# A last norm applied to rows, loads reordered, and weight preparation spread over the first two turns of a fused transformer kernel

## The reference, cut to what matters

```python
h = patches(x) @ tok_W.T + tok_b                 # 32 x 196 rows of 192
h = concatenate([h, txt], axis=1)                # 32 x 324 rows of 192
h = h + causal_rope_attention(norm(h), Wq, Wk, Wv)
z = norm(h)
xn = norm(z) * norm1_w + norm1_b
q, k, v = split(xn @ qkv_w.T + qkv_b)            # 12 heads of 16
x = z + softmax(q k^T / 4) v @ proj_w.T + proj_b
xn2 = norm(x) * norm2_w + norm2_b                # the last norm
gates = softmax(top2(xn2 @ w_gate))              # 8 experts
out = h + x + sum over e of gates_e * (gelu(xn2 @ W1_e + b1_e) @ W2_e + b2_e)
```

## Time and profile before

| | |
|---|---|
| median of 3 runs | 2673.45 us (2668.47 to 2679.84) |
| profiled execution | 2668.14 us |
| its span in the profile | 2666.3 us |
| PE matmul busy | 2423.8 us, 91% of the span |
| DVE busy | 1622.4 us, 61% |
| ACT busy | 1161.3 us, 44% |
| POOL busy | 1043.8 us, 39% |
| mean granted PE clock | 0.934 |

### The profile page before, as it was taken

How to read it: one execution, slowest core, us unless ns; L and a number is a source line. 1 busy time by engine, 2 the same in 40 slices (tenths; PEclk the granted TensorE clock), 3 DMA queues, 4 the chain that set the end, 5 groups by cost and what they waited for, 6 DMA issues and landing times. The chain is left out here.

```text
span 2666.3 us, 64384 instructions
## 1 busy us (share of the span) xinstructions
PE 2423.8 (91%) x19692; PEld 1880.4 (71%) x19692; DVE 1622.4 (61%) x4054; ACT 1161.3 (44%) x2242; POOL 1043.8 (39%) x1196
## 2 busy tenths in 40 slices
PE   3879999999999999899999999999999877989896
PEld 2755666666666666677777777777777657988886
DVE  2336888888888888866776666766666532111111
ACT  2223433444344434345555555555555532433332
POOL 1101333333333333244444444444444434555455
PEclk9568899999999999999999999999999988999998
DMA  5621123122322132425545555544553336887775
GB/s 97 176 28 21 35 40 49 31 35 36 50 34 32 35 50 38 109 73 116 113 99 106 108 114 115 108 94 103 114 109 103 97 96 198 211 224 201 215 208 127
DMA packets 251814, 263.23 MB, mean 99 GB/s; under 512 B 36156, under 2 KB 231464, under 8 KB 251752
## 3 DMA queue, kind: packets, MB, share of 16 engines
q1 hardware_dynamic: 214888, 230.18, 37.0%
q0 software_dynamic: 36864, 32.27, 6.9%
HBM read 212.43 MB, written 52.83 MB: 99 GB/s over the span
## 5 line engine op out<-in xcount | busy, mean ns | idle before, releaser
L1257 DVE TENSOR_REDUCE MX<-PS 108x2 f32<-108x648 f32 x576 | 455.7, 824 | 61.2 <-PE PS L1690 56.3
L817 POOL DMA_INDIRECT out<-big,tokn x192 | 303.9, 1583 | 479.4 <-DVE big L1408 262.5
L967 ACT ACTIVATE pool<-PS 108x648 f32<-108x648 f32 x576 | 387.6, 714 | 213.6 <-PE PS L1713 186.0
L1569 PE MATMUL PS<-WB,big 128*128 128x192 f32 x2304 | 408.3, 333 | 3.4 <-ACT big L996 3.4
L1569 PE MATMUL PS<-XE,WF 128*128 128x256 f16 x2880 | 369.6, 281 | 40.0 <-DMA WF<-w1p 26.1
L996 ACT ACTIVATE big<-PS,WF 128x256 f32<-128x256 f32 x576 | 242.1, 473 | 374.1 <-PE PS L1569 371.2
L1569 PEld LDWEIGHTS PS<-WB,big 128*128 128x128 f32 x2304 | 377.0, 192 | 28.7 <-issue 18.5
L1569 PEld LDWEIGHTS PS<-XE,WF 128*128 128x128 f16 x2880 | 278.4, 100 | 98.0 <-issue 33.0
L794 POOL DMA_INDIRECT xbuf<-XR,DST x192 | 190.7, 993 | 230.9 <-issue 187.9
L1408 DVE SCALAR_TENSOR_TENSOR big<-PS,grow,GB 128x192 f32<-128x192 f32 x192 | 71.3, 413 | 290.9 <-POOL GB L805 148.9
L1724 PE MATMUL PS<-pool,Vp 108*32 108x324 f32 x2304 | 213.9, 513 | 1.5 <-ACT pool L967 1.5
(11 more groups left out here) (209 smaller groups left out, 4163.7 us busy)
## 6 DMA issues: line engine op xcount, KB each, us to landing
WF<-w1p SPq DMA_DIRECT2D x96, 771.5 KB, 5.1
WB<-in_L_ffn_W SPq DMA_DIRECT2D x96, 576.0 KB, 6.0
ximg<-in_x SPq DMA_DIRECT2D x96, 196.0 KB, 5.3
XtR<-xbuf SPq DMA_DIRECT2D x96, 196.0 KB, 2.6
ximg<-in_x SPq DMA_DIRECT2D x96, 195.1 KB, 8.6
B2t<-in_L_ffn_b SPq DMA_DIRECT2D x96, 96.0 KB, 7.0
out<-R SPq DMA_DIRECT2D x32, 243.0 KB
w1p<-WF SPq DMA_DIRECT2D x8, 768.0 KB, 5.5
```

What stands on the lines that cost most here:

```text
L817: nc.gpsimd.indirect_dma_start(rows_out, bass.IndirectOffsetOnAxis(ap=tokn[:, i, s_:s_ + 1], axis=0), Yt[:, i, s_, :], None, bounds_check= ...
L967: nc.scalar.activation(Pr[:, at:at + 2, :], pair(("st", p))[0:TP, :, 0:T], ACT.Exp, scale=SCALE2).then_inc(S["ex"], 1)
L1257: nc.vector.tensor_reduce(MX[:, qt, g, 64 * jj:64 * jj + 64:32], pair(("s", p))[0:TP, :, 0:T], AX.X, ALU.max).then_inc(S["mx"], 1)
L1569: last = nc.tensor.matmul(out_ap, lhsT, rhs, start=(i == 0), stop=(i == len(products) - 1))
```

## The change

Four things. (1) The last norm's scale and offset are applied in `n3` to the rows, in two passes with a wait between them; W1, the gate weights and `b1` stay as they are, and PE's sums and `gateb` go. (2) SP issues the first loads in another order, with a semaphore for each use in place of two for all; the image and the text of batch 0 come early. (3) Preparation moves into the turns: turn 0 holds the attention weights (`early`), the six parts of `qkv_w` (`preps`), the round trip of the bias (`ready`), W1 parts 0 to 7 and, as its last step, the projection (`proj`); turn 1 holds W1 parts 8 to 15. The bias sums on DVE stand right before turn 0. (4) Raw weights land in `WB2` (three slots, and one area for the attention weights) and no longer in `pool1`; the `rsi` buffer becomes single, and part of the expert tables moves to `NB`.

The order of turn 0 is, after the change: emb, he, text, st0, early, is0, n0, tr1, tr1h, tr1l, qk1 0, v1, rm 0, v1e, qk1 1, rs 0, rm 1, rs 1, preps, stage 0, s1, m1, stage 1, e1, p1t, stage 2, rcp, p1e, stage 3, pv1, h1, stage 4, st1, xin, stage 5, is1, n1, stage 6, tr2, tr2h, stage 7, tr2l, hb, ready, qk2 0, xf, qkh 0, qk2 1, qkl 0, qkh 1, v2, qkl 1, qk2 2, qkh 2, qkl 2, v2e, proj. In turn 1 stage 8 stands after the first `s`, 9 before `n0`, 10 before `tr1`, 11 after `tr1l`, 12 before `rm 0`, 13 after `mx 10`, 14 after `st 0`, 15 before `m1`.

```diff
...
                and not (self.last and step in self.plan.ahead)]
-        if isinstance(self.front, int) and self.front == 0:
-            for k in range(2 * E):
-                out.insert(3 * k + 2, ("stage", k))
+        if isinstance(self.front, int) and self.front < 2:
+            if self.front == 0:
+                out.insert(out.index(("st0",)) + 1, ("early",))
+                out.insert(out.index(("s1",)), ("preps",))
+                out.insert(min(out.index(("qk2", 0)), out.index(("v2",))), ("ready",))
+                out.append(("proj",))
+            first = out.index(("s1",)) if self.front == 0 else 2
+            for k in range(E):
+                out.insert(first + (3 if self.front == 0 else 8) * k, ("stage", E * self.front + k))
...
         WB2 = sb("WB2", [128, 3, NC, D], F32)
+        attS = WB2[:, 0, :, :]
+        slot = [WB2[:, 1:3, :, :].rearrange("p r c d -> p (r c d)")[:, HID * i:HID * (i + 1)] for i in range(3)]
...
             def expert_out(e):
-                sp.wait_ge(stg_lo, low_upto(EARLY + 2 * e + 2))
+                sp.wait_ge(stg_lo, 2 * e + 2)
...
+            def bias_in():
+                sp.wait_ge(qb_ready, 1)
+                sp.dma_start(qbd.rearrange("(a p) -> p a", p=96), sred[:, 0:6], allow_slow_non_contiguous=True).then_inc(qb_out, 16)
+                sp.wait_ge(qb_out, 16)
+                for j in range(4):
+                    for a in range(2):
+                        sp.dma_start(qkb[32 * j + HD * a:32 * j + HD * a + HD, :],
+                                     qbd[0:2 * D].rearrange("(i j d) -> j d i", j=4, d=HD)[j],
+                                     allow_slow_non_contiguous=True).then_inc(qb_in, 16)
+                sp.dma_start(vrow, row(qbd[2 * D:], 96)).then_inc(vr_in, 16)
...
                     if step[0] == "stage":
-                        if step[1] + 2 < 2 * E:
-                            stage(EARLY + step[1] + 2)
-                        if step[1] % 2 == 1 and step[1] >= 3:
-                            expert_out(step[1] // 2 - 1)
+                        if step[1] % 2:
+                            expert_out(step[1] // 2)
+                        if step[1] + 3 < NSTG:
+                            stage(step[1] + 3)
+                    elif step[0] == "ready":
+                        bias_in()
                     elif step[0] == "xin":
                         if not (isinstance(item, int) and item == B - 1):
...
+            sp.dma_start(tokS, tok_w.rearrange("(a p) n -> p a n", p=96)).then_inc(tok_in, 16)
+            image(0)
+            sp.dma_start(tokb[:, :], row(tok_b, TP)).then_inc(tokb_in, 16)
+            for n, w in enumerate((wq, wk, wv)):
+                sp.dma_start(attS[:, 2 * n, :], w[0:128, :]).then_inc(att_in, 16)
+                for r in range(2):
+                    sp.dma_start(attS[64 * r:64 * r + 64, 2 * n + 1, :], w[128:D, :]).then_inc(att_in, 16)
+            sp.dma_start(qkvS, qkv_w.rearrange("(a p) n -> p a n", p=96)).then_inc(qkv_in, 16)
+            sp.dma_start(nrow, row(n1b, 96)).then_inc(n_in, 16)
+            sp.dma_start(sred[:, 0:6], qkv_b.rearrange("(a p) -> p a", p=96), allow_slow_non_contiguous=True).then_inc(n_in, 16)
+            sp.dma_start(nw[:, 0:1], column(n1w[0:128])).then_inc(nw_in, 16)
+            for r in range(2):
+                sp.dma_start(nw[64 * r:64 * r + 64, 1:2], column(n1w[128:D])).then_inc(nw_in, 16)
+            text(0)
             sp.wait_ge(pad_set, 1)
-            sp.dma_start(tokS, tok_w.rearrange("(a p) n -> p a n", p=96)).then_inc(big_in, 16)
-            sp.dma_start(qkvS, qkv_w.rearrange("(a p) n -> p a n", p=96)).then_inc(big_in, 16)
...
-            image(0)
-            sp.dma_start(nrow, n1b.rearrange("(a n) -> a n", a=1).to_broadcast([96, D])).then_inc(n_in, 16)
...
-            for i in range(4):
-                stage(i)
...
+            for k in range(3):
+                stage(k)
+            for i, v in enumerate((n2w, n2b)):
+                sp.dma_start(n2[:, i, :], row(v, TP)).then_inc(n2_in, 16)
...
             for e in range(E):
-                const_in(b1s[:, e, 0:NC], b1[e].rearrange("(c p) -> p c", p=128))
...
-            for i in range(4, EARLY + 2):
-                stage(i)
+                sp.dma_start(b1s[:, e, 0:NC], b1[e].rearrange("(c p) -> p c", p=128), allow_slow_non_contiguous=True
+                             ).then_inc(b1_in, 16)
...
-            pool.wait_ge(big_in, 128)
+            pool.wait_ge(tok_in, 16)
...
-            act.wait_ge(c_in, N_C[0])
-            for i in range(len(preps)):
-                v, hi, lo, scale = prep_view(i)
-                act.wait_ge(prep_full, i + 1)
-                nc.scalar.activation(hi, v, ACT.Identity, scale=scale).then_inc(prep_hi, 1)
...
-            for i in range(EARLY):
-                stage(i)
...
+            def prep(kind):
+                if kind == "qkv":
+                    act.wait_ge(nw_in, 48)
+                for i in PREPS[kind]:
+                    v, hi, lo, scale = prep_view(i)
+                    act.wait_ge(prep_full, i + 1)
+                    nc.scalar.activation(hi, v, ACT.Identity, scale=scale).then_inc(prep_hi, 1)
+            def attention_weights():
+                act.wait_ge(att_in, 144)
+                for v, hi, lo in early:
+                    nc.scalar.activation(hi, v, ACT.Copy).then_inc(att_hi, 1)
+            def stage(k):
+                v, hi, lo = stage_views(k)
+                act.wait_ge(stg_in[k % 3], 32 * (k // 3 + 1))
+                if k >= 6:
+                    act.wait_ge(w1_out[k // 2 % 3], 16 * (k // 2 // 3))
+                nc.scalar.activation(hi, v, ACT.Copy, scale=WSC).then_inc(stg_hi, 1)
+            prep("tok")
...
-            dve.wait_ge(big_in, 128)
-            dve.wait_ge(n_in, 48)
...
+            def bias_sums():
+                dve.wait_ge(qkv_in, 16)
+                dve.wait_ge(n_in, 32)
+                set_done(nc.vector.tensor_tensor(sprod.rearrange("p (a n) -> p a n", a=6), qkvS, wide96(nrow, 6), ALU.mult))
+                set_done(nc.vector.tensor_reduce(sred[:, 8:14], sprod.rearrange("p (a n) -> p a n", a=6), AX.X, ALU.add))
+                nc.vector.tensor_tensor(sred[:, 0:6], sred[:, 0:6], sred[:, 8:14], ALU.add).then_inc(qb_ready, 1)
...
                 dve.wait_ge(S["xl"], due("xl", b - 1, 1))
                 for t in range(NT):
-                    last = nc.vector.tensor_scalar(NB[:, t, :], X1[:, t, :], mvb[:, t, 0:1], rsb[:, t:t + 1],
-                                                   ALU.subtract, ALU.mult)
+                    last = nc.vector.scalar_tensor_tensor(NB[:, t, :], X1[:, t, :], mvb[:, t, 0:1], n2[:, 0, :],
+                                                          ALU.subtract, ALU.mult)
+                last.then_inc(S["na"], 1)
+                dve.wait_ge(S["na"], due("na", b, 1))
+                for t in range(NT):
+                    last = nc.vector.scalar_tensor_tensor(NB[:, t, :], NB[:, t, :], rsb[:, t:t + 1], n2[:, 1, :],
+                                                          ALU.mult, ALU.add)
                 last.then_inc(S["n3"], 1)
...
                 dve.wait_ge(S["gate"], due("gate", b, 1))
                 dve.wait_ge(S["pos2"], due("pos2", b - 1, 1))
-                nc.vector.tensor_tensor(L, bank(("gate",))[0:TP, 0:NT * E].rearrange("p (t e) -> p t e", e=E),
-                                        gateb[:, :].rearrange("p (a e) -> p a e", a=1).to_broadcast([TP, NT, E]),
-                                        ALU.add).then_inc(S["logit"], 1)
...
+            bias_sums()
+            dve.wait_ge(tokb_in, 16)
             run(Turn(BOTH, 0, None, None, None))
...
-            pe.wait_ge(nb_ready, 1)
-            for i in (ATT, ATT + 1):
-                pe.wait_ge(stg_in[i % 4], 32 * (i // 4 + 1))
-            nc.tensor.matmul(PS[3][0:TP, 0, 0:E], nbig[:, 0, :], slot[ATT % 4][:, 0:E], start=True, stop=False)
...
-                for c in range(NC):
-                    out_ap = PS[3][:, 1, NC * e + c:NC * e + c + 1]
-                    nc.tensor.matmul(out_ap, slot[i % 4][:, 128 * c:128 * c + 128], nw[:, 4:5], start=True, stop=False)
-                    last = nc.tensor.matmul(out_ap, slot[(i + 1) % 4][0:KB, 128 * c:128 * c + 128], nw[0:KB, 5:6],
-                                            start=False, stop=True)
-                last.then_inc(stg_mm, 1)
...
                     if kind == "stage":
-                        stage(step[1])
+                        continue
...
+                    if kind == "ready":
+                        pe.wait_ge(prep_hi, NQKV)
+                        pe.wait_ge(prep_lo, lows(NQKV))
+                        continue
+                    if kind == "proj":
+                        pe.wait_ge(proj_ready, 1)
+                        prep("proj")
                         continue
...
-            pe.wait_ge(b1_add, 1)
+            pe.wait_ge(prep_hi, len(preps))
+            pe.wait_ge(gate_in, 48)
...
```

(64 more changed lines are left out.)

273 lines of the change are left out of this document (108 added, 165 removed).

## The result

The changed kernel took 2642.59 us in the median of four runs (2635.86 to 2648.85), the kernel before 2671.59 us beside it (four runs, 2668.47 to 2679.84). The ratio is 0.988, 95% interval 0.9851 to 0.9908: faster by 29 us, where 31.8 were forecast (2641.7). Measured a second time, beside eleven runs of the kernel before, the ratio was 0.9902 (0.9882 to 0.9922).

The account below looks back on a forecast made before the run. PE was taken to set the pace in steady turns, but little in the 237 us of start and turns 0 and 1. Terms -33.9 - 2.2 + 2.7 + 1.6 = -31.8 take 2673.45 to 2641.7 us; range 2622 to 2660.

Parts of the forecast that it names:

- Term 1: Start of the kernel: with loads reordered, `he` of turn 0 starts at 28.7 instead of 62.6, -33.9 us.
- Term 2: Turn 0: b1 sums removed, preparations and bias round trip moved in, -2.2 us in sum.
- (a): Turn 0: PE's 192 one-column b1 matmuls go, -24.0 us, bounds -11.7 and -48.6.
- (c): Turn 0's end: the bias round trip waits in SP's DMA queue and stalls `qkh`, +16 us, bounds +10 and +26.
- (b): Turn 0: qkv preparations, `early` and eight W1 parts are mostly hidden, +2 us; with no cover, +8.
- (d): End of turn 0: `proj` exposed, last `qk2` at the lower clock, `b1_add` wait gone: +3.8 us, bounds +1 and +5.
- Term 3: Turn 1: eight W1 parts enter, some of them delaying steps, +2.7 us, bounds 0 and 8.2.
- Term 4: `n3` in 32 batches: +1.35 us each, mostly absorbed by DVE's idle time before `h1`, +1.6 us.
- A: Bias round trip not held up by the queue: stall 10 us or less, about 2630; chance 0.16.
- B: W1 chain lags: parts 4 to 7 each arrive 3 us later, 12 us more, 2654; chance 0.15.
- C: PE stays at 1.2 GHz in turns 0 and 1: +10 us, 2652; chance 0.10.
- D: `n3` decides: its whole 1.35 us passes to PE in 30 turns, 2680, slower; chance 0.04.

Follow-up runs that it names:

- e5: The changed kernel once more, unaltered, with a profile of another execution: 2636.45 us, ratio 0.9902.
- e4: The kernel before, with PE computing only one of the six columns of b1 sums of each expert: 2640.5 us, ratio 0.993.
- e1: The changed kernel with the bias round trip issued right behind the b1 loads, ahead of turn 0: 2618.35 us, ratio 0.9845.
- e9: e1 with the preparation of proj_w also moved, to right ahead of `n1` in turn 0: 2614.0 us, ratio 0.9798.
- e11: e9 with `n3` in one pass, the last norm's scale and offset left out: 2615.51 us, ratio 0.9794.
- e12: e9 with the first pass of `n3` moved ahead of `m1` in the attention turns: 2615.41 us, ratio 0.9791.
- e3: The changed kernel with 16 filler instructions at the head of ACT's program: 2632.81 us in a single execution.
- e8: The changed kernel with the first pass of `n3` done twice: 2646.83 us in a single execution.

## Why the prediction was right

**Term 1, -33.9, measured -34.0** (62.63 to 28.60; the other profiles of kernels with this start have 26.9 to 28.6). Two of its parts were off and cancelled: `emb` starts at 19.9, not 18, for the image landed later; and DVE's sums end at 27.4, not 28.6. So PE set `he`; in e5 the two end within 0.1 us of each other, and `he` starts at 26.9. That the term came out to 0.1 us is luck; its mechanism, loads in the order of use, is what the trace shows. The bound of 26.2 that I gave for hidden sums rested on the 18.

**Term 2, -2.2, measured -6.1**, 88.4 in both profiles of the changed kernel. (a) -24.0 against -26.4 by e4 (20.0 measured, 6.4 estimated); of the 24.0 only the last block's 11.7 had rows behind it. (c) +16 against +15.6, by which `qm` came earlier in e1; its inner times were 76.3 for 80.5 (issue), 14.4 for 13 (the store), 4.8 for 5.5 (the way back). (b) and (d) were never separated in full: with the others measured, -6.1 + 26.4 - 15.6 = +4.7 is left for them where I had 5.8, and 2.1 of it went with the stall in e1 (17.7 us in all). e9 (less the 2.8 us of clock), e11 and e12 put the part of `proj` at 1.2 to 2.6 us.

The queue in front of the store was the reason for (c)'s size, as argued from the earlier trace rows: 7.0, 9.3, 14.4 us with nothing, W1 transfers, and image and W1 transfers ahead. The Trainium skill (DMA: Bandwidth & Descriptors, Queues, rings and completion order) has each DMA engine work through a queue in ring order; by that rule a small store waits for what stands ahead of it, and all three runs agree. But 7.0 of the 14.4 us were there with no large transfer ahead of it, and some 5 passed in all three with the DMA engines idle, so moving the trip, not emptying the queue, is the cure.

**Term 3, +2.7, measured +1.6 in the mean**: turn 1 took 77.9 to 84.5 us in the twelve profiles with eight parts in it, 81.6 in the mean (83.3 and 84.0 for the changed kernel), against 80.0 in the one profile of before. That is too wide to confirm the parts of the term. The scatter is the clock: 78.0 us went with a granted clock of 0.74 and 58.4 us of busy PE (e3), 84.0 with 0.65 and 65.1 (e5).

**Term 4, +1.6, measured some 4 in the attention turns**, and between 0 and 15 us by the ratios of whole kernels: its size is not settled. That DVE's gap takes the pass in was right in each kind of turn, and so were the 0.1 us left over in 16 turns (25.71 for 25.62 us at `h1`), though by two slips that cancel: 1.35 less the gap of 1.17 is 0.18 and not 0.1, and the pass added 1.18. The rest of the 4 us is the mix of clock stretches, which I had not foreseen.

**The sum.** Profile of before to e5's profile the span fell by 31.4 us, nearly the forecast's 31.8, and by 19.3 to the first profile. The medians give 29.0 beside the first measurement and 24.2 beside e5, where the kernel before ran faster (2660.6) than in its profile (2668.1). The terms as measured add up to some -34.5. So the mechanisms of terms 1 and 2, nearly all of the forecast, are shown, and the total to some 5 to 10 us; that 31.8 and 29.0 lie so close is in part luck. The test that I had set, steady turns lengthened by 0.5 us or more, called the prediction wrong on the first profile (55.07 for 54.30) and not on e5's; only the repeat clears term 4.

**The rivals.** A (trip not held up) is excluded by 14.4 against 7.0. B (W1 chain lags, 12 us): with the bias trip out of the way turn 0 took 70.7 us, against 71.5 expected without any lag. C (PE stays at 1.2 GHz): turn 0 and 1 had 0.61 and 0.67, against 0.60 and 0.66; e4, with the sums nearly gone, had 0.63 and 0.73. The Trainium skill (TensorE: Matmul & The Clock Gate, Part 1) has activity release the clock, from which I made rival C; the 48.6 us of one-column matmuls had not raised it here, and without them it was no lower. D would have needed 1.1 us exposed in each of 30 turns; 0.1 was, in the attention turns alone. One pass more (e8) would have exposed 1.0 per turn there, 14.7 us in 15 turns, and nothing in the expert turns. E: the start came forward whole.

**What remains open** is the 0.8 us at `v2e`. Program and inputs are the same with and without it, and in turns of equal clock (the one that starts at 637 us in the first profile, the one at 630 in e5's) so are all starts of PE to 0.1 us up to the last `v2` matmul; the tables of DMA queues show no code transfer in the two turns at 309 to 419 us. It was not tried to produce it at will. Open too is what the second pass costs in the whole kernel.

## What to carry to other kernels

A work item taken off a busy engine is worth the time between "next inputs ready" and "next step starts", and that includes the wait for the item's own load: of 48.6 us of one-column sums and the waits for their loads, some 26 were on the path (20 measured). A round trip through memory must be issued when its data is ready, however small it is, and not where its result is used: here 17.7 us, over half of what the start had gained, were got back by moving one call. That kernel (ratio 0.9845, and 0.9798 with `proj_w`'s preparation moved too) beats both, the changed one being at 0.988 and 0.990. And before a small lengthening of every turn is laid to an edit, the unchanged program should be profiled a second time.

## What the runs showed of the hardware that was not expected

A 2.2 KB store of single 4-byte elements took 7.0 us to land with no large transfer ahead of it, in the kernel before as in e1. In all fourteen profiles 4.8 to 5.7 us of its time lie behind the last packet, with the DMA engines idle; only the rest depends on what stands ahead of it. The eight 0.4 KB loads back took 1.9 us each in the median of e1.

One and the same program had spans of 2647.0 and 2634.9 us. In the longer one ACT took up a finished result 0.92 us after its end, in the other 0.1 us, in all attention turns from turn 3 to turn 16; those turns hold about half of the difference. Three of fourteen profiles show the delay, and in these the expert turns too are longer, 72.3 to 72.7 us for 71.8.

Turn 1's `emb` took 8.9 us at a mean granted clock of 0.61 (the first profile of the changed kernel), 7.5 at 0.72 (e5, the same program) and 5.9 at 1.00 (e9): this alone moves the time of a kernel by up to 3 us without an edit.
